# A two-layer graph network on one core: second norm, features and sums turned in 64-row halves, a value product moved ahead of the aggregation, and the loops over the graphs written out

## What is computed

```
h = relu(layernorm(x))
q, k, v = heads(h @ Wq + bq), heads(h @ Wk + bk), heads(h @ Wv + bv)     # 6 heads of 64
probs = softmax(q @ k^T / 8 + (0 if adjacent else -9e15))
x = x + (probs @ v) @ Wf + bf

h = relu(layernorm(x))
f = einsum("bnd,ade->bane", h, W); th = tanh(f)                          # 12 heads of 32
attn = softmax(where(adj, leaky_relu(th @ w_src + (th @ w_dst)^T), -999))
feat = elu(attn @ f + b)
gate = sigmoid(h @ H_w^T + H_b)
x = x + gate * feat + (1 - gate) * h
```

## Time and profile before

| | |
|---|---|
| median of 3 runs | 1798.44 us (1798.32 to 1798.64) |
| the profiled execution | 1799.47 us, span 1797.7 us |
| mean granted PE clock | 0.99 of full speed |
| PE, DVE, ACT, POOL busy | 93%, 74%, 61%, 58% |
| transfers | 46.46 MB, 26 GB/s over the span |

### The profile page before, as it was taken

One profiled execution on the slowest core, in us unless ns is written; L12 is line 12 of the kernel. 1 busy time (PEld: TensorE's weight loads), 2 busy tenths in 40 slices (PEclk: granted clock), 3 DMA queues, 4 the chain that ended last, 5 costly groups with the idle time before them and its releaser, 6 DMA issues.

```text
span 1797.7 us, 39493 instructions
## 1 busy us (share of the span) xinstructions
PE 1674.6 (93%) x12528; PEld 1021.2 (57%) x12528; DVE 1335.1 (74%) x3130; ACT 1101.8 (61%) x2231; POOL 1033.7 (58%) x1287
## 2 busy tenths in 40 slices
PE   5899999999999999999999999999999999999885
PEld 4464655647465574645657465574655646556461
DVE  4778687786878768677786877768777786876847
ACT  2666566665666656566665666666566665666653
POOL 4356565674656656565564646646565565655735
PEclk9899999999999999999999999999999999999998
DMA  4000101001010010100001010010100101000000
GB/s 155 19 19 12 49 6 35 18 14 44 6 51 7 13 39 6 53 6 21 32 10 48 6 35 23 9 44 6 53 6 13 39 9 50 6 18 19 10 10 18
DMA packets 38114, 46.46 MB, mean 26 GB/s; under 512 B 2624, under 2 KB 38080, under 8 KB 38080
## 3 DMA queue, kind: packets, MB, share of 16 engines
q1 hardware_dynamic: 38080, 46.03, 8.0%
HBM read 33.44 MB, written 12.58 MB: 26 GB/s over the span
## 4 chain that ended last, share of the span: by engine, by line
PE 72%; ACT 12%; DVE 8%; issue 6%; POOL 1%; DVEq 1%; DMA 0%; ACTq 0%; POOLq 0%
PE work L1099 16%; PE score L1099 16%; ACT arena L576 8%; PE acc L1258 8%; PE acc L1252 6%; PE acc L1190 5%; PE score L1156 4%; DVE arena L867 4%; PE work L1173 3%; PE work L1252 3%; PE score L1233 2%; PE acc L1211 2%; ACT arena L582 2%; PE score L1219 1%; PE work L1271 1%
## 5 line engine op out<-in xcount | busy, mean ns | idle before, releaser
L867 DVE SCALAR_TENSOR_TENSOR arena<-score,uqT,adjT 128x512 f32<-128x512 f32 x576 | 389.1, 744 | 35.7 <-PE score L1233 25.4
L416 POOL TENSOR_SCALAR arena<-arena,rinv 128x512 f32<-128x512 f32 x384 | 280.4, 746 | 185.8 <-DVE rinv L828 185.8
L576 ACT ACTIVATE arena<-sm,nmax 128x512 f32<-128x512 f32 x384 | 273.1, 713 | 128.8 <-DVE nmax L822 126.8
L450 POOL TENSOR_TENSOR arena<-arena,adjT 128x512 f32<-128x512 f32 x192 | 224.0, 1167 | 126.0 <-ACT arena L617 121.7
L822 DVE CUSTOM_DVE_ANT_0 sm<-score,mask 128x512 f32<-128x512 f32 x384 | 247.7, 685 | 60.4 <-PE score L1156 57.9
L1173 PEld LDWEIGHTS work<-ident_f,arena 64*128 64x128 f32 x3072 | 115.2, 140 | 185.9 <-issue 185.9
L1258 PE MATMUL acc<-arena,u_den 128*3 128x512 f32 x1536 | 200.8, 592 | 0.0
L1190 PE MATMUL acc<-arena,v_tok 128*64 128x512 f32 x768 | 198.7, 617 | 0.0
L423 POOL TENSOR_TENSOR rstd<-var,mhalf 128x1 f32<-128x1 f32 x128 | 68.7, 549 | 225.6 <-DVE var L786 225.6
L1173 PE MATMUL work<-ident_f,arena 64*128 64x64 f32 x3072 | 138.0, 229 | 60.5 <-ACT arena L582 40.9
L614 ACT ACTIVATE arena<-score,nqT 128x512 f32<-128x512 f32 x192 | 130.0, 677 | 103.3 <-PE score L1233 75.8
(11 more groups left out here) (168 smaller groups left out, 3952.2 us busy)
## 6 DMA issues: line engine op xcount, KB each, us to landing
x_in<-in_x SPq DMA_DIRECT2D x16, 768.0 KB, 4.6
xb<-in_x SPq DMA_DIRECT2D x16, 768.0 KB, 4.5
out_x<-xres SPq DMA_DIRECT2D x64, 192.0 KB, 1.9
adj_u<-in_adj SPq DMA_DIRECT2D x16, 256.0 KB, 2.8
arena<-in_wk SPq DMA_DIRECT2D x1, 576.0 KB, 6.1
arena<-in_wq SPq DMA_DIRECT2D x1, 576.0 KB, 7.2
arena<-in_wv SPq DMA_DIRECT2D x1, 576.0 KB, 8.5
arena<-in_wf SPq DMA_DIRECT2D x1, 576.0 KB, 9.5
```

Of the source, the lines that this page charges most:

```text
L416: nc.gpsimd.tensor_scalar(pr, pr, rinv[:, p, t, i:i + 1], 1.0, ALU.mult, ALU.mult).then_inc(probs_ready, 1)
L450: nc.gpsimd.tensor_tensor(edge_at(n, HG - 1), t_ring[:, n % 2], adjT[:, n % TT], ALU.mult).then_inc(last_edge_ready, 1)
L576: nc.scalar.activation(probs[p % 2 * 2 + i][:, t], sm[:, n % NSM], ACT.Exp, scale=-1.0, bias=nmax[:, p, t, i:i + 1], accum_out=rsum[:, p, ...
L867: nc.vector.scalar_tensor_tensor(out=edge_at(n, j), in0=score[j][:], scalar=uqT[:, c, q:q + 1], in1=adjT[:, c], op0=ALU.max, op1=ALU.mult) ...
```

## The change

Five things are changed.

- *Half transposes.* The second norm, the features and the sums are turned two row tiles at a time, in 64-row halves (`turn_halves`). One half of the rows of both tiles goes to one bank, the other half to another. Two whole tiles of three blocks become twelve half transposes; two row tiles of the sums, with four blocks each, become 32. ACT's and DVE's copies from these banks (`turned_high2`, `turned_low2`, the copy of `tok`, `inverse_den`, `divide`) read one half of two tiles instead of one whole tile. The second norm's copies no longer repeat the ReLU.
- *Heads.* Which four heads form an aggregation group is reordered (`head_of`), so that the heads of one half lie side by side.
- *Value products.* The first one of the next graph moves from behind group 5 to the place ahead of group 0, the second from the end to behind group 5. Value products alternate between banks 0 and 1, and so do the sums. ACT copies the first value behind its maxima of group 1, and the gate's tanh of tiles 1 to 3 move to groups 2, 3 and 6.
- *The end of the layer.* PE's order is now: scores (0,0), group 11, scores (0,1), sums 0 and 1, scores (0,2), value 2, scores (0,3), value 3, sums 2 and 3, scores (1,0). DVE's and ACT's orders follow.
- *Loops.* The loops over the graphs are written out on all engines.

The core of the diff:

```diff
-    ("v", 0): 1, ("v", 1): 1, ("v", 2): 1, ("v", 3): 0,
+    ("v", 0): 0, ("v", 1): 1, ("v", 2): 0, ("v", 3): 1,
...
-    ("num", 1): 0, ("fin", 0): 0, ("fin", 1): 0, ("fin", 2): 1, ("fin", 3): 1,
+    ("num", 1): 0, ("fin", 0): 0, ("fin", 1): 1, ("fin", 2): 0, ("fin", 3): 1,
...
 (ACT, layer2)
                 for n in range(STEPS):
                     last_maxima(b, n)
-                    if n < 3:
-                        tanh_gate(b, n + 1)
+                    if more and n == 1:
+                        value(b + 1, 0)
+                    if n in TANH_AT:
+                        tanh_gate(b, TANH_AT[n])
...
                     if more and n == 8:
-                        value(b + 1, 0)
+                        value(b + 1, 1)
                 if more:
                     exps(b + 1, 0, 0)
                 sums_copy(b, NG - 1)
                 if more:
-                    value(b + 1, 1)
                     exps(b + 1, 0, 1)
                     value(b + 1, 2)
                     exps(b + 1, 0, 2)
+                    value(b + 1, 3)
                     exps(b + 1, 0, 3)
-                    value(b + 1, 3)
                     exps(b + 1, 1, 0)
...
 (DVE, layer2)
                 nc.vector.tensor_copy(denT, acc[1][:]).then_inc(den_drained, 1)
-                for t in range(TT):
-                    if more and t < TT - 1:
-                        maxima(b + 1, 0, t + 1)
-                    if more:
-                        inverse(b + 1, 0, t)
-                    inverse_den(b, t)
-                    divide(b, t)
-                if more:
+                if more:
+                    maxima(b + 1, 0, 1)
+                    inverse(b + 1, 0, 0)
+                for m in range(2):
+                    inverse_den(b, m)
+                    divide(b, m)
+                if more:
+                    maxima(b + 1, 0, 2)
+                    inverse(b + 1, 0, 1)
+                    maxima(b + 1, 0, 3)
+                    inverse(b + 1, 0, 2)
+                for m in range(2, 4):
+                    inverse_den(b, m)
+                    divide(b, m)
+                if more:
+                    inverse(b + 1, 0, 3)
                     maxima(b + 1, 1, 0)
...
 (PE)
+            def turn_halves(banks, blocks, source):
+                for t in range(2):
+                    for c in range(blocks):
+                        for half in range(2):
+                            rows = slice(half * DH0, (half + 1) * DH0)
+                            at = (t * blocks + c) * DH0
+                            ins = nc.tensor.transpose(banks[half][0][:, at:at + DH0], source(t, c)[rows],
+                                                      ident_f[rows, rows])
+                            if (t, c) == (1, blocks - 1):
+                                mark_full(ins, *banks[half][1])
...
+            def turn_norm2(b, pair):
+                for half in range(2):
+                    bank_free(pe, b, "norm2", 2 * pair + half)
+                pe.wait_ge(hn_ready, b * TT + 2 * pair + 2)
...
-                turn_norm(b, 1, 0)
-                turn_norm(b, 1, 1)
+                turn_norm2(b, 0)
                 if more:
                     query_key(b + 1, 0, "q")
-                turn_norm(b, 1, 2)
-                turn_norm(b, 1, 3)
+                turn_norm2(b, 1)
...
                 gate_product(b, 3)
+                if more:
+                    values(b + 1, 0)
...
                     if more and n == 5:
-                        values(b + 1, 0)
+                        values(b + 1, 1)
...
                 if more:
                     scores(b + 1, 0, 1)
-                    values(b + 1, 1)
                 turn_sums(b, 0)
                 if more:
                     scores(b + 1, 0, 2)
                     values(b + 1, 2)
+                    scores(b + 1, 0, 3)
+                    values(b + 1, 3)
                 turn_sums(b, 1)
                 if more:
-                    scores(b + 1, 0, 3)
-                turn_sums(b, 2)
-                if more:
-                    values(b + 1, 3)
-                turn_sums(b, 3)
-                if more:
                     scores(b + 1, 1, 0)
...
-            with pe.Fori(0, B - 2) as b:
+            for b in range(B - 2):
```

More of the change, by code:

```diff
@@ L190, in view @@
                 return v
-            names_ = "abc"[:len(shape)]
+            names_ = "abcd"[:len(shape)]
             return v.rearrange("p (%s) -> p %s" % (" ".join(names_), " ".join(names_)),
@@ L326, in tile_no, with halves, turned @@
             return (p * TT + t) * 2 + i
+        def halves(tensor, m):
+            pair, half = m // 2, m % 2
+            return tensor[:, :, pair * 2 * P:(pair + 1) * 2 * P].rearrange(
+                "p c (t h n) -> p t c h n", t=2, h=2)[:, :, :, half]
+        def turned(bank_, blocks):
+            return bank_[:, 0:2 * blocks * DH0].rearrange("p (t c n) -> p t c n", t=2, c=blocks)
         block = ctx.enter_context(nc.Block())
@@ L386, in turn @@
                     next_x(b + 2)
-            with sp.Fori(0, B - 3) as b:
+            for b in range(B - 3):
                 turn(b, True, True)
@@ L545, in norm2, with turned_high1, turned_high2 @@
                                      bias=shift[:, 1, t:t + 1], scale=rstd[:, 1, t:t + 1]).then_inc(hn_ready, 1)
[L547 to L552, removed]
+            def turned_high1(g, t):
+                filled(act, g, "norm1", t)
+                nc.scalar.activation(hT_hi[0][:, :, t * P:(t + 1) * P],
+                                     bank_of(g, "norm1", t)[:, 0:D].rearrange("p (c n) -> p c n", c=FC),
+                                     ACT.Relu).then_inc(hi_ready[0], 1)
+            def turned_high2(b, m):
+                filled(act, b, "norm2", m)
+                nc.scalar.activation(halves(hT_hi[1], m), turned(bank_of(b, "norm2", m), FC),
+                                     ACT.Copy).then_inc(hi_ready[1], 1)
             def qk_hi_copy(g, p, name):
@@ L754, in _ @@
             attention(0, True, False)
-            with act.Fori(0, B - 2) as b:
+            for b in range(B - 2):
                 layer2(b, True)
@@ L1074, in _ @@
             norm2(0, True)
-            with dve.Fori(0, B - 2) as b:
+            for b in range(B - 2):
                 layer2(b, True, True)
@@ L1214, in logits, with turn_feat @@
                     ins.then_inc((logits_b_full, logits_full)[c - 1], 1)
[L1216 to L1221 removed]
+            def turn_feat(b, pair):
+                for half in range(2):
+                    bank_free(pe, b, "tok", 2 * pair + half)
+                settle(pe)
+                turn_halves([(bank_of(b, "tok", 2 * pair + half), (b, "tok", 2 * pair + half)) for half in range(2)], FC,
+                            lambda t, c: feat[:, c, (2 * pair + t) * P:(2 * pair + t + 1) * P])
             def spread(b, g, j):
@@ L1267, in turn_sums @@
                     pe.wait_ge(den_drained, b + 1)
-                bank_free(pe, b, "fin", t)
-                ps = bank_of(b, "fin", t)
-                for g in range(NG):
-                    nc.tensor.transpose(ps[:, g * P:(g + 1) * P], numT[:, g, t * P:(t + 1) * P], ident_f[:])
-                mark_full(nc.tensor.transpose(ps[:, D:N], denT[:, t * P:(t + 1) * P], ident_f[:]), b, "fin", t)
+                for half in range(2):
+                    bank_free(pe, b, "fin", 2 * pair + half)
+                settle(pe)
+                turn_halves([(bank_of(b, "fin", 2 * pair + half), (b, "fin", 2 * pair + half)) for half in range(2)], NG + 1,
+                            lambda t, c: (numT[:, c] if c < NG else denT)[:, (2 * pair + t) * P:(2 * pair + t + 1) * P])
             def attention(g, more):
@@ L1314, in layer2 @@
                     drained(pe, b, "feat", c)
-                for t in range(TT):
-                    turn_feat(b, t)
+                for pair in range(2):
+                    turn_feat(b, pair)
                 gate_product(b, 0)
```

139 lines of the change are left out of this document (74 added, 65 removed).

## The result

The changed kernel takes 1805.10 us (median of 6 runs, 1804.04 to 1806.41), the kernel before 1798.59 beside it (6 runs, 1798.32 to 1799.73): ratio 1.0035, 95% interval 1.0023 to 1.0047. It is slower, as forecast, but by 6.5 us where 26.6 were forecast.

What follows compares the result with a forecast made beforehand. PE was taken as nearly full (93% busy), with the softmax chain beside it at the layer's end. 1.65 + 0.25 - 0.1 = 1.8 us in each of 15 transitions, 27 us, gave 1825; range 1807 to 1842.

Steps and rivals of the forecast that it cites:

- end of the layer: Last aggregation group to first turned probabilities: +15.4 instead of +13.77, 1.65 us later per graph, bounds 0.9 and 2.4.
- shift up to the aggregation: Last aggregation group starts 0.25 us later: value product +0.45, features -0.3, norm +0.1; bounds 0 and +0.5.
- loops: Writing the loops out saves 0.1 us a graph, between -0.35 and 0; instruction fetching costed at nothing.
- start and end of the program: The ends of the program, outside the 15 transitions between graphs, were taken as unchanged.
- the mechanism at the end of the layer: Second sums pair waits for value 3's copy; then DVE's divisions, row tile 3's reciprocal, POOL, PE: 1.65 us later.
- two pairs of 32 halves, 1.30 each: End of the layer: the four turns of the sums become two pairs of 32 half transposes, 1.30 us each.
- PE does not stay the bound: Rival: PE work alone bounds the layer's end, 11.5 instead of 13.77 us; 31 us faster, 1768; chance 0.13.
- rival three: Granted clock falls as PE idles 2.6 us ahead of the turned probabilities; 26 us more, 1851; chance 0.05.
- The halves cost half: Rival: by the skill's tiling rule a tile in halves costs 0.053 instead of 0.081 us; 1807; chance 0.04.
- Back edges cost today: Rival: the loops' 14 back edges cost instruction fetches; writing them out gives back 21 us, 1804; chance 0.03.
- Fetching shows: Rival: some 80 more instruction packets at 1.5 us, near 1945 if none hidden, part likelier; chance 0.02.
- Delay swallowed in the attention: Rival: idle ACT and DVE time takes up the delay, +0.15 a graph remains, 2 us, 1801; chance 0.07.

Runs made afterwards that it cites:

- e1: The kernel before with only its loops written out, on all engines: 1788.44 us, ratio 0.9945.
- e4: The changed kernel with score group (1,1) computed twice more and thrown away, ahead of the turned probabilities, to keep PE busy: 1800.39 us, ratio 1.0010.
- e12: The whole change with the loops kept on all engines: median 1845.05 us, ratio 1.0260; its profiled execution took 1821.91.
- e14: A further profiled execution of the program of e12, the whole change with the loops kept: 1821.35 us.
- e15: A second further profiled execution of the program of e12, the whole change with the loops kept: 1847.57 us.
- e6: The changed kernel with the second pair of sums and score group (1,0) ahead of value product 3, now in bank 0: 1775.84 us, ratio 0.9874.
- e2: The changed kernel with DVE's reciprocal for row tile 3 ahead of the second pair's divisions: 1799.60 us, ratio 1.0003.
- e3: The changed kernel with each pair of sums turned twice, 32 half transposes per pair: 1813.64 us, ratio 1.0084.
- e9: The kernel before with VectorE's loop alone written out: 1792.11 us, 95% interval of the ratio 0.9955 to 0.9979.
- e5: The kernel before with loops written out and value products moved, whole transposes and the old order of the sums: 1775.42 us, ratio 0.9876.
- e7: The version of e5 with the second norm and features in half transposes, sums whole and in the old order: 1770.30 us, ratio 0.9845.
- e8: The changed kernel with both row tile 3's reciprocal first and PE kept busy by two thrown-away score groups: 1787.84 us, ratio 0.9941.

## Why the prediction was wrong in size

Its terms, 15 transitions each, beside what the runs gave:

| term | forecast, us | measured, us | from |
|---|---|---|---|
| end of the layer | +24.8 (1.65) | +10.4 (0.69) | 14.52 - 13.83, after against e1 |
| shift up to the aggregation | +3.8 (0.25) | +3.0 (0.20) | +0.53, -0.31 and -0.02, same |
| loops | -1.5 (0.1) | -10 | e1 against the kernel before |
| clock | 0 | +4.7 | after against e4 |
| start and end of the program | 0 | -1.5 | first adjacency 96.58 against 97.84, tail 71.76 against 72.03, after against e1 |
| sum | +27.1 (26.6 on record, against the median) | +6.6 | measured +6.5 |

The last term is one execution against one: the first adjacency of one program came at 96.97, 95.82 and 96.82 (e12, e14, e15), so it is not resolved.

**Right: the mechanism at the end of the layer.** Every wait that was named is there, in the order named; e6 takes value product 3 and its copy out of the chain, e2 the divisions ahead of the last reciprocal; they give 1.63 and 0.85 us a graph.

**Wrong: the size of that term.** The failed step is "two pairs of 32 halves, 1.30 each". A pair is 2 tiles x 4 blocks x 2 halves, so 16, and they take 0.49 where 64-row score products follow. 0.65 was read ahead of a 128-row product; the kernel before shows the 0.49 too, from the turned probabilities at 925.30 to this row:

```profile
925.79 0.51 PE L1156 MATMUL score<-qk_hi 64*128 64x512 f32 x2
```

Link by link, the forecast and then the rows: the second pair starts at +10.5 and +10.34; from there to DVE's first step 1.30 and 0.72; DVE's four steps 1.66 and 1.48; from the last reciprocal to the turned probabilities 1.87 and 1.97. That adds up to +15.3 (+15.4 on record) and +14.51. e3 prices the count alone at 0.52, and with that count the kernel takes 1813.64, inside the stated range. The other differences were read from rows; no run separates them. The term, 0.69, lies under its own lower bound of 0.9.

**Wrong: "Loops written out ... I take -0.1 a graph".** The evidence was in the profile: graph 14, written out, showed 2.03 against 2.27 between the first two groups. The prediction argued that the moved product fills that stall anyway, and it does; but the other 0.4 a graph lies in the second norm and around the back edge, where it looked only for fetching, not for register instructions between DVE's short steps (e9). Alone, the loops gave 10 us. In the new order they cost more: 17 in e12's profiled execution, which refetched nothing, of which the longer stage up to group 0 is 7.8 and the clock about 5; and about 40 at e12's median, whose executions were not profiled; e15, which refetched, took as long. The bound of -0.35 was too tight.

**Right in sum, by luck: the shift.** 0.20 of 0.25. The moved value product costs 0.60 (e5 against e1: +0.93, -0.31, -0.02) where the forecast had 0.45, and halves of norm and features give 0.38 together (e7 against e5: 25.65, 26.03) where it had 0.2. The two misses cancel.

**The rivals.** PE does not stay the bound: it stands idle for 2.70 ahead of the turned probabilities. The clock does fall, where rival three put it, but it costs 4.7 and not 26: a graph where it fell 13 us behind the last group lost 1.1, one where it fell 16 behind it 0.2. "The halves cost half" gave 1807, close to the result, but mostly for other reasons. In front of a score group two halves cost 0.061 against 0.107 for a whole transpose, nearer to half than the 0.081 of the sum; but 0.65 against 0.49 is 0.16 a pair, and the rest came from the count, the loops and the clock. "Back edges cost today" is refuted for the kernel before (TensorE's loop is worth 2.0, not 21) and came true in some executions of the changed order with its loops kept. "Fetching shows" is refuted: 107 packets, and PE has no wait on issue over 0.2 but the one ahead of the second pair, which stands 0.1 behind value 3's copy; e1, with 102 packets, is 10 us faster. Delay swallowed in the attention: refuted, e2 and e8 move the turned probabilities and the time follows, 12.6 for 0.85 x 15 = 12.8.

**What of the change helps.** Value products in front +13.0 us faster, half transposes of norm and features 5.1, loops 10; turning the sums in halves, with value product 3 ahead of the second pair and the last reciprocal behind its divisions, undoes all of it and 6.5 more: 34.8 us from e7 to the change, of which 4.7 are the clock's. In the one other order that was run, halves of the sums gain nothing either: e6 ends the layer at +12.89, whole turns at +12.48 (e7).

## What to carry to other kernels

Multiply out a loop nest before pricing it: tiles x blocks x halves, checked against the count of instructions on the page. When two tiles share a pair of banks, ask what else sits in these banks: the pair waits for the later of the two, and everything behind it on the next engine (here a reciprocal whose exponentials had ended 0.9 us before) waits with it. When a loop is written out, price each engine's register instructions between its short dependent steps. Price it in the new order too: the loops cost 10 us in the old order, 17 in one execution of the new one and about 40 at its median.

## What the hardware showed that was not expected

- The same program, with a PE loop body of 1830 recorded instructions, refetched at none, 4 or all 13 of its back edges in three executions: 1821.9, 1821.4 and 1847.6 us. What decides it stays open.
- More work made a kernel faster: 12 further matmuls a graph kept the granted clock at 1.00 and saved 4.7 us (e4) and 11.8 (e8 against e2).
- An earlier release of PE's work can be eaten by the clock: e2 brought the turned probabilities 0.85 us forward and lost 7 of 12.7 us to longer stretches at half speed.
- Sixteen 64-row transposes take 0.49 us in front of another 64-row product and 0.65 in front of a 128-row one.
